# The output projection of a fused attention and expert layer: from full-precision products to three products of rounded parts

## The reference, cut to what matters

```python
scores = q @ k.T / sqrt(64)            # per sequence and head, causal mask
attn = softmax(scores); out = attn @ v # 16 heads x 64 columns
y = out_concat @ Wo + bo               # (256, 1024) @ (1024, 128)
x = layernorm(x + y)
...
xn = norm(x) * gamma + beta            # router, top 2 of 8 experts, silu MLP
x = layernorm(x + experts(xn))
```

## Time and profile before

| | |
|---|---|
| three runs, us | 1309.6, 1308.0, 1307.06; median 1308.0 |
| profiled execution, span | 1306.0 us (the page gives no other time for it) |
| PE busy | 1284.0 us, 98% |
| PE's granted clock | 0.999 of full speed |
| DVE busy | 1098.7 us, 84% |
| ACT busy | 1078.0 us, 83% |
| POOL busy | 508.6 us, 39% |
| one sequence, input's transposes to the next ones | 31.0 to 31.1 us |

### The profile page before, as it was taken

The page is one execution under the profiler, slowest core; times in us unless marked ns, Lnnn a source line. Parts: engine busy times, 40 slices in busy tenths (PEclk is TensorE's granted clock), DMA queues, the critical chain, the costliest instruction groups (busy, mean ns, idle before and its releaser), DMA issues.

```text
span 1306.0 us, 36164 instructions
## 1 busy us (share of the span) xinstructions
PE 1284.0 (98%) x11298; PEld 1139.8 (87%) x11298; DVE 1098.7 (84%) x5201; ACT 1078.0 (83%) x3481; POOL 508.6 (39%) x1075
## 2 busy tenths in 40 slices
PE   7999999999999999999999999999999999999997
PEld 6888888888888888888888888888887999999983
DVE  6888888888888888888888888888887898888847
ACT  7888888888888888888888888888887777777737
POOL 1024333333333333333333333333333676565645
PEclk9999999999999999999999999999999999999999
DMA  5000100100000000000000000000023687777749
GB/s 212 18 22 30 34 30 33 34 32 14 14 14 14 14 14 14 14 14 15 14 14 14 14 14 18 17 16 16 16 110 125 178 236 232 232 232 228 223 133 338
DMA packets 58860, 98.19 MB, mean 75 GB/s; under 512 B 9376, under 2 KB 36131, under 8 KB 58416
## 3 DMA queue, kind: packets, MB, share of 16 engines
q1 hardware_dynamic: 49024, 78.67, 19.3%
q0 software_dynamic: 8640, 17.13, 3.8%
q10 hardware_dynamic: 1008, 0.08, 0.1%
HBM read 65.85 MB, written 30.91 MB: 74 GB/s over the span
## 4 chain that ended last, share of the span: by engine, by line
PE 91%; DVE 3%; ACT 2%; DMA 1%; issue 1%; SPq 0%; POOL 0%; POOLq 0%; ACTq 0%; DVEq 0%
PE ps_f L1116 16%; PE ps_b L1150 14%; PE ps_a L1116 14%; PE ps_s L1157 13%; PE ps_s L1138 10%; PE ps_s L1116 7%; PE ps_a L1348 4%; PE ps_b L1348 4%; PE ps_s L1141 4%; PE ps_s L1418 2%; PE ps_a L1190 1%; PE ps_f L1182 1%; PE ps_s L1162 1%; ACT probs L608 1%; DMA m_x<-queue 1%
## 5 line engine op out<-in xcount | busy, mean ns | idle before, releaser
L608 ACT ACTIVATE probs<-probs,neg_max 128x256 f32<-128x256 f32 x512 | 255.4, 499 | 128.7 <-DVE neg_max L859 128.7
L855 DVE CUSTOM_DVE_ANT_0 probs<-ps_s,mask 128x256 f32<-128x256 f32 x512 | 214.4, 419 | 32.1 <-PE ps_s L1141 29.7
L474 POOL TENSOR_SCALAR ln_b<-mv 128x2 f32<-128x2 f32 x32 | 6.0, 188 | 500.6 <-DVE mv L922 500.6
L1157 PE MATMUL ps_s<-ident,probs 128*128 128x128 f32 x1536 | 199.7, 274 | 0.0
L610 ACT ACTIVATE probs<-probs,neg_max 128x128 f32<-128x128 f32 x512 | 198.7, 388 | 0.0
L1150 PE MATMUL ps_b<-pt,f_y 128*64 128x256 f32 (+1 forms) x2048 | 194.7, 332 | 1.6 <-issue 0.9
L869 DVE TENSOR_SCALAR probs<-probs,inv_sums 128x256 f32<-128x256 f32 x512 | 182.3, 356 | 9.1
L573 POOL DMA_INDIRECT y_tok<-f_y,m_dest x142 | 145.7, 1026 | 84.2 <-DVE m_dest L1022 57.6
L1150 PEld LDWEIGHTS ps_b<-pt,f_y 128*64 128x64 f32 x2048 | 131.6, 137 | 51.4 <-issue 6.7
L1138 PE MATMUL ps_s<-qk 64*128 64x256 f32 x1024 | 170.6, 409 | 5.0 <-ACT qk L598 1.9
L1157 PEld LDWEIGHTS ps_s<-ident,probs 128*128 128x128 f32 x1536 | 172.3, 142 | 0.4 <-issue 0.3
(11 more groups left out here) (208 smaller groups left out, 3151.1 us busy)
## 6 DMA issues: line engine op xcount, KB each, us to landing
m_w<-w_split SPq DMA_DIRECT2D x71, 512.0 KB
m_x<-queue SPq DMA_DIRECT2D x71, 133.0 KB
f_y<-y_tok SPq DMA_DIRECT2D x32, 256.0 KB, 6.3
queue<-empty SPq DMA_DIRECT2D x8, 532.0 KB
x_raw<-in_x SPq DMA_DIRECT2D x32, 128.0 KB, 2.1
w_split<-f_y SPq DMA_DIRECT2D x8, 512.0 KB, 2.6
out_x<-f_y SPq DMA_DIRECT2D x16, 256.0 KB, 6.5
y_tok<-f_y,m_dest POOLq DMA_INDIRECT x142
```

Of the source, the lines that this page charges most:

```text
L608: act.activation(row[:, 0:2 * P], row[:, 0:2 * P], ACT.Exp, scale=-1.0, bias=neg_max[:, pair, h, 0:1], accum_out=sums[:, d % 2, pair, h, 0:1])
L855: dve.tensor_tensor_reduce(out=row[:, 0:2 * P], in0=ps_s[:, pair, h, 0:2 * P], in1=mask[:].rearrange("p a b -> p (a b)"), scale=-1.0, scal ...
L1157: ins = pe.transpose(ps_s[:, pair, h, dst:dst + P], probs[:, buf, pair, h, src:src + P], ident[:])
```

## The change

- **Operands.** `wo` is split into `wo_hi` and `wo_lo` once by POOL at the start (`split_projection`). Each step's attention outputs are copied by ACT into one of two small buffers of `ot` (it held two sequences before) and POOL then makes `ot_hi` (a copy, rounded) and `ot_lo` (a subtraction), 512 columns each (`split_outputs`). ACT's next copy but one waits for it. The split of step q = 2's copy stands in q = 3 between `norm` and `residual_input`, that of q = 3's copy in q = 0 of the next sequence, and those of q = 0's and q = 1's copies both in q = 1.
- **Product.** The output is transposed: `wo` parts are stationary, `ot` parts moving, 256 columns each; eight chunks times three terms, in two halves of twelve. Half 0 is PE's second filler in q = 1, half 1 its first filler in q = 2. ACT copies the result from PSUM to `out_t`, and PE transposes it back in two pieces. DVE adds `xb` to both tiles in one instruction and takes the statistics right after.
- **Orders.** The input's transposes and their split move from q = 2 to q = 1. In q = 2 PE's `qk_projection` of pair 1 moves behind the transposes of the probabilities, to the end of the step. `copy_outputs` in q = 1 and 2 moves to the end of ACT's step. DVE's `second_pt` moves ahead of the second `normalise` in q = 1 and behind the residual in q = 2. `send_tokens(n)` moves from q = 3 of n to q = 0 of n + 1. `probs` moves into the memory that `ot` gave free.

```diff
-        def projection_at(n, i):
-
-            return ps_f[:, 0:D] if n < SEQS else ps_f[:, i * D:(i + 1) * D]
+        def projection_at():
+
+            return ps_f[:, S:S + TILES * D].rearrange("p (i d) -> p i d", i=TILES)
...
+            def split_outputs(d):
+                n, first = (d - 2) // QUADS, (d - 2) % QUADS * 2
+                pool.wait_ge(ot_done, d - 1)
+                if n >= 1:
+                    pool.wait_ge(out_half_ready, 2 * n - (1 if first < 4 else 0))
+                pool.tensor_copy(ot_hi[:, first:first + 2, :], ot[:, d % 2]).then_inc(ot_hi_done, 1)
+                pool.wait_ge(ot_hi_done, d - 1)
+                pool.tensor_tensor(ot_lo[:, first:first + 2, :], ot[:, d % 2], ot_hi[:, first:first + 2, :].bitcast(F32),
+                                   ALU.subtract).then_inc(ot_lo_done, 1)
...
             def step(n, q, d):
+                if q == 0 and n in MID:
+                    split_outputs(d - 1)
+                if q == 0 and n - 1 in LATE:
+                    send_tokens(n - 1)
+                if q == 1 and n in MID:
+                    split_outputs(d - 1)
+                    split_outputs(d)
                 if q == 1 and 1 <= n <= E:
                     rest_of_w1(n - 1)
                 if q == 3 and n in MID:
                     norm(n)
-                if q == 3 and n < SEQS:
+                if q == 3:
+                    split_outputs(d - 1)
                     residual_input(n)
-                if q == 3 and n in LATE:
-                    send_tokens(n)
 
             pool.wait_ge(small_loaded, 16 * 5)
+            split_projection()
             sequences(step)
+            split_outputs(LAST - 1)
+            split_outputs(LAST)
+            split_outputs(LAST + 1)
+            send_tokens(SEQS - 1)
             norm(SEQS)
             send_tokens(SEQS)
...
             def copy_outputs(d):
-                par, first = (d - 2) // QUADS % 2, (d - 2) % QUADS * 2
                 act.wait_ge(o_ready, d - 1)
-                act.activation(ot[:, par, first:first + 2, :].rearrange("p c t -> p (c t)"), ps_b[:], ACT.Copy
-                               ).then_inc(ot_done, 1)
+                if d >= 4:
+                    act.wait_ge(ot_lo_done, d - 3)
+                act.activation(ot[:, d % 2].rearrange("p c t -> p (c t)"), ps_b[:], ACT.Copy).then_inc(ot_done, 1)
+
+            def copy_projection(n):
+                act.wait_ge(out_half_ready, 2 * n)
+                if n >= 2:
+                    act.wait_ge(proj_ready, n - 1)
+                act.activation(out_t[:], ps_f[:, 0:S], ACT.Copy).then_inc(out_t_done, 1)
...
+                if q == 2 and n in MID:
+                    copy_projection(n)
...
-                if d == LAST - 1:
+                if d == LAST - 1 or (q == 1 and n in MID):
                     second_pt(d)
                 if d < LAST:
                     normalise(d, 1)
-                if 1 <= d < LAST - 1:
+                if q == 2 and n in MID:
+                    residual(n)
+                    second_pt(d)
+                    statistics(n)
+                if 1 <= d < LAST - 1 and (q in (0, 3) or n == 0):
                     second_pt(d)
...
-            def output_projection(n, i):
-                par = (n - 1) % 2
-                product(projection_at(n, i), [(ot[:, par, c, i * P:(i + 1) * P], wo_sb[:, c, :]) for c in range(PAIRS)]
-                        ).then_inc(proj_ready, 1)
+            def output_projection(n, half):
+                for c in range(half * PAIRS // 2, (half + 1) * PAIRS // 2):
+                    if c % 2 == 0:
+                        pe.wait_ge(ot_lo_done, (n - 1) * QUADS + c // 2 + 1)
+                    for k, (lhs, rhs) in enumerate(split_terms(wo_hi[:, c, :], wo_lo[:, c, :],
+                                                               ot_hi[:, c, :], ot_lo[:, c, :])):
+                        ins = pe.matmul(ps_f[:, 0:S], lhs, rhs, start=(c == 0 and k == 0),
+                                        stop=(c == PAIRS - 1 and k == 2))
+                ins.then_inc(out_half_ready, 1)
+
+            def transpose_projection(n):
+                pe.wait_ge(out_t_done, n)
+                for i in range(TILES):
+                    ins = pe.transpose(projection_at()[:, i, :], out_t[:, i * P:(i + 1) * P], ident[:])
+                ins.then_inc(proj_ready, 1)
...
+                if q == 2 and n in MID:
+                    first_transposes(d)
+                    transpose_projection(n)
+                if d + 1 < LAST and (q != 2 or n == 0):
                     qk_projection((d + 1) // QUADS % 2, (d + 1) % QUADS * 2 + 1, 1)
...
+                if q == 2 and n in MID:
+                    qk_projection((d + 1) // QUADS % 2, (d + 1) % QUADS * 2 + 1, 1)
                 second_filler(n, q)
```

More of the change, by code:

```diff
@@ L651, in step @@
                         exponentials(d, 0, h)
[L652 to L658, removed]
+                if q == (1 if n >= 1 else 2) and n + 1 < SEQS:
+                    round_input(n)
                 if d == LAST - 1:
@@ L680, in step @@
                     evacuate_qk(d + 1, 1)
[L681 removed]
+                if 2 <= d < LAST - 1 and q >= 1:
                     copy_outputs(d)
@@ L690, in step @@
                     evacuate_second_v(n * 4 + 2, 0)
-                if q == 3 and n < SEQS - 1:
+                if q == (3 if n < SEQS - 1 else 1):
                     evacuate_second_v(n * 4 + 4, 1)
@@ L731, in _ @@
                 keep(j)
+                if j == 0:
+                    copy_projection(SEQS)
                 if j == 2:
@@ L977, in step @@
                     normalise(d, 0)
+                if q == (1 if n >= 1 else 2) and n + 1 < SEQS:
+                    if n == 0:
+                        rest_of_xt(2, 1)
+                    else:
+                        rest_of_xt(n + 2, (n + 1) % 2)
                 if n in LATE:
@@ L984, in step @@
                     dve.tensor_tensor(bo_sb[:], ps_f[:, 0:D], bo_sb[:], ALU.add).then_inc(bo_done, 1)
-                if q == 2 and n + 1 < SEQS:
-                    rest_of_xt(n + 2, (n + 1) % 2)
                 if q == 0 and 1 <= n < SEQS:
@@ L995, in step @@
                     evacuate_first_v(n * 4 + 3, 1)
-                if d == LAST - 1:
+                if q == 2 and n in LATE:
+                    places(n)
+                if d == LAST - 1 or (q == 1 and n in MID):
                     second_pt(d)
@@ L1005, in step @@
                     router_difference(n)
-                if q == 2 and n in LATE:
-                    places(n)
-                if q in (1, 2) and n in MID:
-                    residual(n, q - 1)
             sequences(step)
@@ L1075, in _ @@
                 if j == 0:
-                    for i in range(TILES):
-                        residual(SEQS, i)
-                    variance(SEQS, 2)
-                    variance(SEQS, 3)
+                    residual(SEQS)
+                    statistics(SEQS)
+                    variance(SEQS)
                     router(SEQS, 1)
@@ L1251, in step @@
                             pe.wait_ge(r_diff_done, n - 1)
-                        if pair == 1 and q == 3 and n in LATE:
-                            pe.wait_ge(ranks_done, n - 1)
                         scores(pair)
@@ L1384, in _ @@
                     transpose_x(1)
-                    pe.wait_ge(ot_done, LAST)
-                    for i in range(TILES):
-                        output_projection(SEQS, i)
+                    for half in range(2):
+                        output_projection(SEQS, half)
+                    transpose_projection(SEQS)
                 if j == 2:
```

120 lines of the change are left out of this document (71 added, 49 removed).

## The result

The changed kernel takes 1328.8 us (median, 1326.4 to 1329.2, 4 runs), the kernel before 1307.9 us beside it (4 runs). The ratio is 1.0152, 95% interval 1.0138 to 1.0166: slower by 1.5%, with a forecast of 1334. A second measurement gave 1330.7 against 1308.5, 1.0167 [1.0152, 1.0182].

A forecast was written before the change was run, and what follows sets the result against it. PE, busy 98% of the span, was taken as the bound. PE's gain of 0.61 and a stall of 1.3 us made +0.7 a sequence, +22 in all, plus 4 at the end: 1334 us, range 1318 to 1352.

The forecast's parts named there:

- PE: Projection and transposes back take 3.15 us for 3.76 removed, so PE gains 0.61 us a sequence.
- The late pair: qk_projection's second pair, last in q = 2, makes PE wait about 0.3 us in q = 3; bounds 0 to 0.6.
- The collision: POOL's split in q = 3 blocks DVE's second normalisation, making it 1.7 us later; bounds 0 and 2.4.
- the margin: From q = 3 to q = 0, DVE's PSUM copy ends 0.39 us before PE starts the second pair of scores.
- The splits in q = 1: First split ends near 3.7 us, just when DVE's first normalisation starts; costed at nothing, bounds 0 and 1.2 us.
- the stall: PE waits in q = 0 for DVE's late copy: 1.7 less 0.39, 1.3 us a sequence, late pair's wait included.
- ACT, SP, sends: ACT's added 0.36 us PSUM read, SP's later x loads and the moved sends cost nothing in the sequences.
- The end: Three splits and the sends stand before the last norm, so z and y sends come late: +4 us once, bounds 0 and 8.
- The sum: Per sequence -0.61 + 1.3 = +0.7 us, times 31 = +22, and +4: span 1306.0 becomes 1332, forecast 1334.
- Rival B: Last split of q = 1 also hits DVE's normalisation, delaying q = 2: +1.7 us a sequence, 1365 us; chance 0.17.
- Rival A: PE's gain comes through, as POOL doesn't hold DVE fully or the q = 3 split misses: 1298 us; chance 0.33.
- Rival C: One half of the split hits, 0.6 us, and PE's gain and the stall cancel: 1308 us; chance 0.07.

The follow-up runs named there:

- the gates: Changed kernel with POOL's split in q = 3 and both in q = 1 waiting for DVE's normalisations (three waits); 1316.4 us against 1308.5 before.
- one gate: Changed kernel with only POOL's split in q = 3 waiting for DVE's second normalisation; 1416.4 us against 1394.6 for the kernel before.
- the two tries at the end: The gated kernel with the last z transposes to token send one expert block later, 1314.6 us; or its last three splits on ACT and DVE, 1308.0.
- the gated kernel: Kernel with the gates, plus transposes back behind the late qk_projection and residual behind second_pt; 1312.8 us against 1308.5 for the kernel before.
- the last gated kernel: The gated kernel with the last three splits on ACT and DVE instead of POOL; 0.9768 of the kernel before, 0.9988 in a later run.

## Why the prediction was right

**PE.** Forecast -0.61 us a sequence, measured -0.48 (q = 1 and q = 2 together). The halves take 1.54 us with their switch, so the projection takes 3.08, and 3.30 with the transposes back, for the 3.15 forecast.

**The late pair.** Forecast 0.3 us of wait in q = 3, measured 0.24, with q = 3 longer by 0.34. The 0.25 us that I had added for signals stands in no row; it is 0.16 here, as ACT's first read starts 0.11 us behind the first scores (440.42) and PE follows the end of the second read by 0.05. The wait lay inside DVE's delay, as forecast: taken away alone it brought nothing, taken away behind the gates it brought 0.18 us a sequence.

**The collision.** The mechanism, its place and its victim were right, and the Trainium skill's rule that the one who comes second is blocked for the whole instruction (SBUF — State Buffer, section "Who interferes with whom") holds here for 1.28 us as it did for 0.46: an L917 of 1.37 us beside a subtraction of 1.28. The size was off. In q = 3 of a steady sequence DVE's normalisations last some 1.65 us over their undisturbed lengths, and 0.25 before: 1.4 us added. The delay that reaches `second_pt` is 1.14 us (it starts 8.05 us behind q = 3's first scores, 6.91 before), where I had 1.7. Of it 0.34 is covered by the longer q = 3 and 0.39 by the margin; what is left, 0.4, is near the 0.54 us that PE loses ahead of the second pair. One part of the difference is the split's copy: 0.61 us, not 0.9, and it held the multiplication at 445.83 by 0.09 us where I had 0.3. My bound from below (0.5, from the memset) was nearer. The 0.77 us of the Trainium skill (GPSIMD Engine Reference, section 3.1) was nearer too.

**The splits in q = 1.** I put nothing on the first one, since it would end near 3.7 us, just when the normalisation starts. It ends at 3.75, and the normalisation starts at 3.76. That was right by 0.01 us and so by luck: with one gate, where the stall ahead of it is gone, the same split hits in 18 of 20 sequences.

**ACT, SP, sends.** Nothing forecast, nothing seen: ACT's copy of the projection is 0.36 us and ends ahead of PE's need, and the sends alone cost nothing.

**The end.** Forecast +4, measured +3.3 behind the last scores (5.5 in the second profile), with 2.4 in sequence 31, where I had 0.7. The reason given (z and the y sends late behind splits and sends) is the one that the two tries at the end bear out. In the gated kernel, whose last steps are quicker, POOL's queue cost 5.8 us, more than PE's wait for z alone.

**The sum.** +0.43 for +0.7 a sequence, and so 18.6 us of span for 26. The forecast of 1334 was 5 us high, and the mis-sized term is the stall: 0.91 (0.57 in q = 0, 0.34 in q = 3) in place of 1.3.

**Rival B** did not happen in the changed kernel, though its mechanism is real: two kernels show it at 1.5 to 1.6 us a sequence as soon as the stall in q = 0 is taken away (I had taken 1.0, half of a hit of 2 us). My condition, a DVE lag of 0.3 us, was reached only without the stall that I forecast beside it, by way of the first split of q = 1: the forecast and B exclude each other, and I had added B's hit to the forecast's stall. **Rival A** (1298) isn't reached where the collision with the normalisations is gone: with three gates it is 1316.4, since q = 3's late pair, the held cast with DVE's lag in q = 2 and the end remain, and PE's gain is 0.48. No run is free of every collision. **Rival C** took the right sort of stall at half its size.

## What to carry to other kernels

An idle engine isn't free to take work: GpSimd had 60% of its time left, but its copies and subtractions on SBUF held back VectorE's multiplications from SBUF to SBUF, and one small cast, until they were through. So the place of such work matters, not its load. Put it beside VectorE's PSUM reads, with a wait on the semaphore that VectorE's SBUF work already sets. Then look at what it stands beside now, however small: the gate that freed the normalisations here put a split beside a cast of four columns, which then took 1.01 us instead of 0.17. When a stall is removed, look at what it kept apart, and at a kernel's end add up the serial queue of the engine that sends.

## What the runs showed of the hardware

- GpSimd rounds 128x512 from f32 to fp32r in 0.61 us, and subtracts as many in 1.28 (means 614 and 1283 ns over 128 each). VectorE does that subtraction in 0.68 to 0.69 us when undisturbed.
- VectorE's 128x128 multiply of 0.28 us took 1.37 us beside such a subtraction, and a 128x4 cast of 0.17 us took 1.01; its maxima from PSUM kept their 0.41 and 0.28 us beside the splits early in q = 0.
- Not every SBUF instruction of VectorE was held: with the gates, a FIND_INDEX8 that starts 0.09 us behind the subtraction keeps its 0.16 us, and the router's reduction and MAX8 beside the copy keep 0.16 and 0.23.
- In two groups of runs the kernels that were also measured elsewhere took some 55 to 85 us longer. The versions with gates lost less there than the kernel before (0.9845 and 0.9768 of it, where elsewhere they have 1.0061 and 0.9988). There is no trace of the kernel before from these groups, but its twin with the later sends has sequences of 32.27 us there for 31.05, the extra in q = 0 and q = 1, and the last gated kernel 31.14 for 30.98. In such a q = 0 DVE and ACT sit idle for 1.82 and 1.34 us and start again at the same time, with no semaphore behind it. Why is open.
